# Eighteen numbers of a tick table: side steps of a six-layer decoder stand at other ticks

## What is computed

```python
def step(t, p):
    tn = _ln(t, norm_g, norm_b)
    t = _mha(tn, tn, skv, sq, sow, sob, tgt_mask) + t      # 16 heads of 64; q 512, k 512
    tn = _ln(t, norm_g, norm_b)
    t = _mha(src, tn, ckv, cq, cow, cob, src_mask) + t     # 16 heads; keys are 77 context tokens
    tn = _ln(t, pg, pb)
    t = t + (jax.nn.relu(tn @ w1 + b1) @ w2 + b2)          # 128 -> 512 -> 128
    return (t, None)
```

## Time and profile before

| what | value |
|---|---|
| median of 3 runs | 1062.11 us (1061.4 to 1063.75) |
| profiled execution | 1062.09 us, span 1060.0 us |
| granted TensorE clock over the span | 0.998 of full speed |
| PE busy | 1025.4 us (97%), 5236 instructions |
| ACT busy | 811.6 us (77%) |
| DVE busy | 717.0 us (68%) |
| POOL busy | 393.8 us (37%) |
| chain of work that ended last | PE 86%, DVE 8%, issue 3%, ACT 1% |
| DMA | 32.39 MB, mean 31 GB/s |

### The profile page before, as it was taken

How to read it: one execution, slowest core, us unless ns; L and a number is a source line. 1 busy time by engine, 2 the same in 40 slices (tenths; PEclk the granted TensorE clock), 3 DMA queues, 4 the chain that set the end, 5 groups by cost and what they waited for, 6 DMA issues and landing times.

```text
span 1060.0 us, 20691 instructions
## 1 busy us (share of the span) xinstructions
PE 1025.4 (97%) x5236; PEld 615.5 (58%) x5236; DVE 717.0 (68%) x4485; ACT 811.6 (77%) x3540; POOL 393.8 (37%) x407
## 2 busy tenths in 40 slices
PE   8899999999999999999999999999999999999996
PEld 6655556565456665545655555656655566555565
DVE  4766786556788566778665578655678755677845
ACT  4787997576998576899666799766799867689852
POOL 4233443233443233443333344323344323344322
PEclk9999999999999999999999999999999999999999
DMA  8322000003000002200003200001300000000000
GB/s 235 88 61 68 1 21 2 1 20 109 20 21 1 2 1 80 68 2 21 1 2 80 68 1 21 1 1 33 103 14 21 2 1 1 21 1 1 2 1 24
DMA packets 31818, 32.39 MB, mean 31 GB/s; under 512 B 3998, under 2 KB 27726, under 8 KB 30926
## 3 DMA queue, kind: packets, MB, share of 16 engines
q1 hardware_dynamic: 29390, 28.80, 9.4%
q10 hardware_dynamic: 2304, 2.20, 0.7%
HBM read 30.47 MB, written 0.52 MB: 29 GB/s over the span
## 4 chain that ended last, share of the span: by engine, by line
PE 86%; DVE 8%; issue 3%; ACT 1%; DVEq 1%; POOL 1%; POOLq 0%
PE S L1090 23%; PE T L1102 12%; PE sum L1132 10%; PE W L901 8%; PE sum L1116 7%; PE W L956 4%; PE W L925 4%; PE W L843 3%; PE W L880 3%; PE W L863 2%; PE W L858 2%; PE W L920 2%; DVE XN L1468 2%; DVE Pb L1620 2%; PE W L834 2%
## 5 line engine op out<-in xcount | busy, mean ns | idle before, releaser
L1382 ACT ACTIVATE Pb<-Pb,mn 128x128 f32<-128x128 f32 (+1 forms) x1536 | 560.5, 370 | 42.4 <-DVE mn L1620 42.1
L708 POOL TENSOR_TENSOR Pb<-Pb,rsum 128x512 f32<-128x512 f32 (+2 forms) x336 | 325.4, 971 | 582.3 <-DVE rsum L1628 582.3
L1382 ACT ACTIVATION_READ_ACCUMULATOR Pb<-Pb,mn 128x1 f32 x1536 | 293.0, 191 | 0.0
L1620 DVE CUSTOM_DVE_ANT_0 Pb<-S,late_bias 128x128 f32<-128x128 f32 x768 | 175.6, 285 | 130.4 <-PE S L1090 130.1
L1102 PEld LDWEIGHTS T<-ident,Pb 128*128 128x128 f32 (+2 forms) x1296 | 163.9, 146 | 155.1 <-issue 119.7
L1090 PE MATMUL S<-GV,XT 128*128 128x512 f32 x384 | 199.6, 607 | 1.6 <-DVE mn L1620 0.8
L1102 PE MATMUL T<-ident,Pb 128*128 128x128 f32 (+2 forms) x1296 | 197.4, 273 | 1.2 <-POOL Pb L708 1.2
L1638 DVE COPY PT<-T 128x512 f32<-128x512 f32 (+1 forms) x240 | 156.3, 651 | 57.1 <-PE T L1102 55.7
L1620 DVE CUSTOM_DVE_ANT_0 Pb<-S,cross_bias 128x77 f32<-128x77 f32 x768 | 132.4, 232 | 70.4 <-PE S L1090 68.0
L1132 PE MATMUL sum<-PT,Vc 128*128 128x512 f32 (+2 forms) x264 | 134.4, 599 | 0.0
L1090 PE MATMUL S<-Gc,XT 128*128 128x462 f32 (+1 forms) x288 | 126.7, 521 | 0.6 <-DVE mn L1620 0.5
(11 more groups left out here) (213 smaller groups left out, 1071.1 us busy)
## 6 DMA issues: line engine op xcount, KB each, us to landing
sakv<-in_L_xattn_sa_kv SPq DMA_DIRECT2D x6, 1024.0 KB, 5.0
caq<-in_L_xattn_ca_q SPq DMA_DIRECT2D x6, 512.0 KB, 8.0
saq<-in_L_xattn_sa_q SPq DMA_DIRECT2D x6, 512.0 KB, 6.2
cakv<-in_L_xattn_ca_kv SPq DMA_DIRECT2D x12, 256.0 KB, 7.8
saow<-in_L_xattn_sa_ow SPq DMA_DIRECT2D x6, 512.0 KB, 4.0
w<-in_L_xattn_ff_w SPq DMA_DIRECT2D x12, 256.0 KB, 3.0
caow<-in_L_xattn_ca_ow SPq DMA_DIRECT2D x30, 96.0 KB, 2.5
GV<-in_mask_BxSxS_ik ACTq DMA_DIRECT2D x1, 1536.0 KB, 9.3
```

The costliest lines, as they stand in the source:

```text
L708: nc.gpsimd.tensor_tensor(rows, rows, r, ALU.mult).then_inc(sem(f"{unit.name}_weights"), 1)
L1382: last = nc.scalar.activation(Pb[:, s, t * w:(t + 1) * w], Pb[:, s, t * w:(t + 1) * w], ACT.Exp, bias=mn[:, s, t:t + 1], scale=-1.0, accum ...
L1620: last = nc.vector.tensor_tensor_reduce(out=Pb[:, s, cols], in0=S_ps[n % 2][:, cols], in1=row_bias, scale=1.0, scalar=3.4e38, op0=ALU.add, ...
```

## The change

Eighteen numbers of the tables differ, on eight lines; the code that reads them is the same.

```diff
-CV0_AT = (13, 15, 18, 20, 26, 30)
-CV_AT = (4, 6, 7, 22, 26, 29)
-SELF1_AT = (23, 25, 26, 30)
+CV0_AT = (10, 12, 15, 16, 24, 27)
+CV_AT = (4, 6, 7, 20, 26, 29)
+SELF1_AT = (23, 24, 26, 30)
 SELF0_AT = (18, 18, 26, 29)
-WEIGHTS0_AT = (5, 3, 7, 10, 13, 16)
-WEIGHTS_AT = (20, 25, 30, 32, 33, 33, 35, 35, 38, 38, 40, 40, 43, 42, 45, 45)
-AFTER_S0 = (3, 4, 5, 5, 8, 9)
+WEIGHTS0_AT = (5, 3, 7, 12, 16, 18)
+WEIGHTS_AT = (20, 23, 30, 32, 33, 33, 35, 35, 37, 37, 40, 40, 43, 42, 45, 45)
+AFTER_S0 = (3, 4, 5, 5, 6, 7)
 AFTER_S1 = (2, 3, 4, 4, 5, 6)
 AFTER_X0 = (2, 2, 3, 4, 5, 7)
 AFTER_X1 = (0, 2, 3, 4, 5, 7)
-LAST_AT = (1, 3, 5, 7)
+LAST_AT = (1, 3, 5, 9)
 FEED0 = ((8, 8, 9, 9), 10, (13, 14, 15, 17))
-FEED1 = ((9, 9, 9, 9), 10, (18, 18, 20, 21))
+FEED1 = ((9, 9, 9, 9), 12, (18, 18, 20, 21))
```

## The result

| what | before | after |
|---|---|---|
| median of the runs | 1062.01 us, 6 runs (1061.04 to 1063.75) | 1057.36 us, 6 runs (1056.28 to 1060.40) |
| ratio, 95% interval | | 0.9956 [0.9940, 0.9972] |
| profiled execution | 1062.09 us, span 1060.0 | 1057.01 us, span 1054.9 |

The change makes the kernel 0.44% faster, by more than this measurement's 0.2%. The forecast was 1058.6, in a range of 1056.0 to 1062.4. So the sign and the cause were foretold, and the size was too small by a third: 3.5 us forecast, 5.1 measured between the two profiled executions.

A forecast was written before the change was run, and what follows sets the result against it. PE's stream was taken as the bound, so only its waits could pay. Per layer 0.20 + 0.60 - 0.15 = 0.65 us, 3.25 in five, plus 0.3 for layer 1: 3.5 off 1062.09, so 1058.6, range 1056.0 to 1062.4.

The forecast's parts named there:

- `out`, forecast 0.20 net: s0, layers 1 to 5: `out` two ticks later removes a 0.40 us loss at scores; 0.20 given back (0 to 0.40).
- What is late next is the addition itself: s0: the addition of `out`, 0.69 us, precedes the next reciprocal and mask; PT copy and PE's next `o` wait, 0.20.
- `cV`, forecast 0.60: s0, layers 1 to 5: `cV` ahead of `xn` hides a 0.70 us hole, less 0.10 for XN slipping.
- my own lower end: `cV` in s0: chain slips by the whole 0.69 addition, less the 0.20 by which `cV` exceeds the hole; 0.21 gained.
- `G`, forecast -0.15: s0, five times: `G` ahead of both `o` saves 0.10, but the second `o` waits 0.25 for `G`'s bank (+0.10 to -1.8).
- The slower rival, a wait of 1.9: s0: exponentials on ACT start only as `G` ends, so the second `o` waits 1.9 us; 1066.8 us, chance 0.10.
- Layer 1's extra 0.3: Layer 1's s0: its longer wait for XN, 0.9 against 0.5 us, adds 0.3 us of gain.
- my bound of 6.3 us: Forecast's best end: all waits gone, nothing given back, 1.2 a layer, 6.0 in five, with layer 1's 0.3: 1055.8 us.
- Moves costed at nothing: s1, x1, `tq` 1, layer 0 and last-layer scaling: no cost; layer 0 0.2 either way, x1 0.2 at worst.
- given back by the norm's chain: s0 rival: DVE sets when `xn` can go; 0.40 is lost again, XN slips 0.69; 1061.5 us, chance 0.14.
- Nothing of it is reached: Rival: PE's stream has a limit the rows do not show, so the change is neutral; 1062.1 us, chance 0.10.
- What would show it: Signs in s0, layers 1 to 5: no POOL wait, prompt `xn`, second `o` waits 0.2 to 0.5, 0.4 to 1.0 shorter.

The follow-up runs named there:

- e7: Kernel before with the moves of `out`, fourth `cV` and first `G`, plus the ck/cv 1 pair one tick later in x1: 1060.22 us, ratio 0.9985.

## Why the prediction was right, and where its sizes were off

**The bound: right.** PE's stream set the time, and a move paid by what PE had waited for. Every microsecond gained is in the s0 of layers 1 to 5.

**`out`, forecast 0.20 net (0.40 less 0.20): the gain right, the give-back at another place.** The 0.40 went, also alone. "What is late next is the addition itself" held, but the sentence after it, that the PT copy and PE's next `o` would wait, did not: T to `o` is 0.59 before and after. The 0.20 came back as a later XN: the addition used up the gap of 0.48 on DVE that I should have read ahead of the copy of `o`, and DVE had nothing left with which to follow a PE that no longer waited. With `cV` in place it cost nothing, so the term was 0.40 in this change.

**`cV`, forecast 0.60 (0.70 less 0.10 of slip): measured 0.70.** The slip was real, and at 0.20 larger than charged. The step that failed is the subtraction: a slip costs nothing while `cV`, 0.90, is longer than the hole of 0.70. I had subtracted a slip from a hole that had 0.20 of cover over it, although my own lower end used that cover. Both terms together were to give 0.80 and gave 1.10.

**`G`, forecast -0.15 with a wait of 0.25: measured +0.03 in layer 3 of the change, and in layers 1 to 5 within 0.05 of nothing alone.** The mechanism I weighed was there with about 0.1 us to spare. What failed is the last step of the working, 0.35 in three terms (the overlap of ACT's copies, PE's arrival, and the signal's 0.15, which no run shows at this place); ACT's starts were right. The 0.10 to be saved was not there either: it moved to the scores behind `o`. The slower rival, a wait of 1.9, had nothing to stand on: exponentials started at 580.24 in the kernel after, 0.7 us before `G` began on PE. They took the place in ACT's queue that I gave them in arguing against it.

**Layer 1's extra 0.3: measured 0.03.** Layer 1 gains 1.10 against 1.07 on average of the other four. Its hole was 1.02 (from 243.33 to 244.79, less the 0.44) and is 1.22 now with `out`; `cV` covers 0.90 of it, and 0.32 remain (a wait of 0.2 in the profile). With `cV` alone layer 1 was ahead by 0.17 (0.90 against 0.73). With `out` moved too, the other layers' hole is 0.90, the whole of `cV`, and nothing is left to be ahead by. A filler can't gain more than its own length. My sum kept to that (0.60 + 0.3), but my bound of 6.3 us did not: it gave layer 1's `cV` 1.0.

**Moves costed at nothing: nearly right.** s1 0.00, the cross stages +0.09 in all. Layer 0's s0 +0.18 was inside its 0.2 either way. Waits that the profile shows aren't all of it. Jobs that change neighbours between full and half-size weights (see the last section) show 0.1 each way, and one chunk's scores that stood behind `cG` and took 0.96 up to their T (53.82 to 54.79) now stand behind a T and take 1.17 (52.59 to 53.76). What they wait for there I have not settled.

**The sum.** Forecast 3.25 + 0.3 = 3.5. Measured 5.37 in the five s0, less 0.18 in layer 0 and 0.09 in the cross stages: 5.1. Of the 1.5 us between, `out` and `cV` make 1.2 (5.5 in five layers without `G`, against 0.80 a layer and 0.3), `G` 0.6 (0.1 lost against 0.75), and the stages costed at nothing take back 0.3. So three terms were too low and two too high (layer 1's extra and the stages at nothing, 0.3 each), and only that little of the error cancelled. **The rivals**: "given back by the norm's chain" named the right mechanism, and alone, without `cV`, `out` does lose half of its gain by it; its prices, 0.40 and 0.69, were too high. "Nothing of it is reached" fell in every layer. **What would show it**: no T waits for POOL (so), `xn` within 0.2 us of the end of `cV` (so, in layer 1 too), s0 shorter by 0.4 to 1.0 (1.03 to 1.13, just outside), all other stages equal to 0.1 (all but layer 0's s0, with 0.18), a new wait at the second `o` (none).

## What to carry to other kernels

Where one engine's stream is the bound, work moved into one of its holes gained here the shorter of the hole and the filler. So a filler a little longer than the hole also pays for a chain that slips a little, and two moves may be worth more together than the sum of each alone. Moving a filler to an earlier hole doesn't help if the chain behind the next hole starts no earlier: ask first what the next wait hangs on. And before work is delayed, look whose bank it must leave: in e7 a hole of 0.9 us was closed at the price of a wait of 1.3.

## What the runs showed of the hardware

A float32 matmul of the program shows as two records in the profile and a transpose as one: one chunk's scores are one matmul in the order of PE above, and x2 in the rows. From start to start a 128x512 matmul takes 0.86 us, and four transposes take 0.44.

The rows give each matmul's weights, 128*128 for most jobs, 128*64 for `o` and 64*128 for `G`. A T is followed by a free job with full weights after 0.44 us (575.54 to 575.98), and by one with half-size weights after 0.53 (580.40 to 580.93 for `G`). Scores behind an `o` took 0.96 to the next start (571.57 to 572.53), where they take 0.86 behind a T. So a pass between the sizes costs up to 0.1 us on PE, with no wait shown. A move that only changes which neighbour pays it brings nothing, as `G` ahead of the `o` pair did.

From the end of what PE waited for to PE's start it is not one figure. `xn` starts 0.15 us behind the end of XN (578.96 to 579.11 before), and `fin` behind ACT's eviction likewise. The T at 571.54 starts 0.06 behind the end of POOL's product (570.44 plus 1.04), and so do scores that waited for a mask. Why they differ no run here tells.

Stages repeated better than I had expected: s1 was 36.52 us, to 0.01, in six layers of all thirteen kernels, while the whole runs of one kernel spread over 0.8 to 5.9 us.
